# Sums over d as two row tiles of 64 partitions in three blocks of four, rows of x0 by transposes, and the fold of a block's partial sums split between GpSimd and VectorE

## The chip, the cores and the metric

The kernel runs on one core of a Trainium2 chip. The metric is the device time of one execution in microseconds (us). TensorE (PE in the rows, its weight loads PEld), VectorE (DVE), ScalarE (ACT), GpSimd (POOL) and the DMA queues each run their own program and meet through semaphores.

## The reference

A recommendation model: 39 embedding rows of 16 numbers for each of 512 samples go through a three-layer cross network, and then through a small perceptron.

```python
e = jnp.stack([tbl_0[ids[:, 0]], ..., tbl_38[ids[:, 38]]], axis=1)   # (512, 39, 16)
x0 = xk = e
for W in (f0, f1, f2):             # (39*39, 128), (128*39, 128), (128*39, 128)
    z = jnp.einsum('bfd,bgd->bfgd', x0, xk).reshape(b, f * g, d)
    cur = jnp.einsum('bpd,pm->bmd', z, W)
    outs.append(cur); xk = cur
z = jnp.sum(jnp.concatenate(outs, axis=1), axis=-1)                  # (512, 384)
h = jnp.concatenate([z, dense_ctx], axis=1)
h = jnp.maximum(h @ W_top1 + b_top1, 0.0)
h = jnp.maximum(h @ W_top2 + b_top2, 0.0)
y = h @ W_top3
```

## The kernel before

A **tile** is 32 samples times 16 values of d, 512 columns; there are 16 tiles. A tile has four **blocks** of 128 columns (8 samples times 16 d), 64 blocks in all. A block's second layer is ten **banks** (a bank is a PSUM buffer y2 of four fields, 512 columns; the tenth has three fields). Each bank is one **slot**, so a tile has 40 slots, numbered 0 to 39 here; slots 40, 41, ... are slots 0, 1, ... of the next tile. Every engine's program is written out along the same slots by hand: an operation's slot is its place in its engine's order, not a time.

In a slot TensorE runs the bank's three matmuls (lines 779 to 781). VectorE multiplies each field of the bank with the field's x0 and adds it to a running sum (line 682, four operations a bank), except for banks 0, 3 and 6 of a block, which ScalarE scales (line 526). There are four y2 buffers, so bank n waits until bank n - 4 has been read. Between the banks lie:

- the next tile's first layer: VectorE's products z = z * three_ps (line 652, at slots 0, 4, ..., 24), their low halves by GpSimd (line 426), TensorE's contraction into acc0 (lines 753, 754 and 759, at slots 8, 12, ..., 32), then x1_low (line 658) and sum_x1 (line 665) by VectorE at slots 35 and 36;
- the rows of x0: four matmuls against the identity a tile (line 743, slot 33), copied by ScalarE;
- the second layer's result of a block: GpSimd adds the three partial sums, fold_two at slot 8 of the block (line 434) and fold_three at slot 2 of the next block (line 441); VectorE adds the four fields of the sum, 128x512 to 128x128, by a reduction, x2_of (line 690) at slot 4 of the next block; TensorE then sums over d with s_block (line 786): the stationary operand is x2 (8 samples x 16 d on the partitions, 128 channels), the moving one is diag, 8 x 40 columns, in which the columns of sample b are nonzero only in b's 16 partitions. It writes 320 columns of the PSUM buffer side, which ScalarE copies to s_sb. s_block stands S_LAG = 18 slots behind its block's first bank, so at slots 8, 18, 28 and 38 of a tile;
- the third layer (line 797) and the perceptron (lines 808, 809, 818 and 825) of the group of four tiles before, from the fifth tile on; the perceptron falls into tiles 7, 11 and 15, counted from 0.

After the last bank the last block's fold, s_block, third layer and perceptron run one after the other.

Of the kernel before, what the change touches and what calls it, by code (L numbers as in the profile page):

```python
# [15 lines left out]
F = 39  # L16
# [5 lines left out]

COLS = 512
BLK = 8
GROUPS = B // P
TPG = 4
TILES = GROUPS * TPG
# [40 lines left out]
BY_ACT = (0, 3, 6)  # L68
FOLD_AT = 8
THIRD_AT = 2  # L70
X2_AT = 4


B_STEP = 4
FIRST_B_AT = 4
HIGH_LAG = 2
LOW_LAG = 3
CONTRACT_LAG = 8
X1_AT = 34
FIRST_X1_AT = 37  # L80
S_LAG = 18

LAST_BLOCKS = (TILES * SLOTS - 2 - S_LAG) // BANKS + 1
ROWS_AT = 33
# [82 lines left out]
    return k // BANKS if k >= 0 and k % BANKS == 0 else None  # L167


def small_fields(tables):  # L170
    return [f for f in range(F) if tables[f].shape[0] <= CHUNKS * ROWS]

# [22 lines left out]
def cross_network(nc, ids, ids_small, row_numbers, small_tables, tables, w0a, w0b, w1, w1_w, w2, wt1, bt1, wt2, bt2, wt3, dense_t, selectors, identity, mask8, out):  # L195
    with ExitStack() as ctx:
# [35 lines left out]

        scaled = sb("scaled", [P, 2, len(BY_ACT), FPB * M])
        sum4 = sb("sum4", [P, FPB * M])
        x2_sb = sb("x2_sb", [P, 2, M])
        diag = sb("diag", [P, 2, NBLK, BLK, FS])
        s_sb = sb("s_sb", [P, 2, FS, P])
# [58 lines left out]
        terms_in = sem("terms_in")  # L296
        y_act = sem("y_act")
        four_in = sem("four_in")
        x2_in = sem("x2_in")
        diag_in = sem("diag_in")  # L300
        s_ready = sem("s_ready")
# [97 lines left out]
        @block.gpsimd  # L399
        def _(pool):  # L400
            def single(g, i):
                f = SINGLES[i]
                if g >= 2 and i == 0:
                    pool.wait_ge(stored[0], 16 * STORES * (2 * (g - 1)))
                    pool.wait_ge(stored[1], 16 * STORES * (2 * (g - 1)))
                pool.indirect_dma_start(
                    out=emb_singles[:, g % 2, i, :], out_offset=None, in_=tables[f][:, :],
                    in_offset=bass.IndirectOffsetOnAxis(ap=ids_sb[:, g, f:f + 1], axis=0),
                ).then_inc(singles_in[g], 16)

            def quad(u, i):
                n = len(QUADS[i])
                if u >= 2 and i == 0:
                    pool.wait_ge(stored[u % 2], 16 * STORES * (u // 2))
                pool.indirect_dma_start(  # L415
                    out=emb_quads[0:SPT * n, u % 2, i, :], out_offset=None, in_=packed,
                    in_offset=bass.IndirectOffsetOnAxis(ap=quad_rows[0:SPT * n, u, i:i + 1], axis=0),
                ).then_inc(quad_in[i][u % 2], 16)

            def low_part(u, c):  # L420
                n = C0 * u + c
                pool.wait_ge(z_hi_in, n + 1)
                if n >= Z_RING:
                    pool.wait_ge(z_done, n - Z_RING + 1)
                k = depth(c)
                pool.tensor_tensor(z_lo[0:k, n % Z_RING, :], z[0:k, c, :], z_hi[0:k, n % Z_RING, :].bitcast(F32),  # L426
                                   ALU.subtract).then_inc(z_lo_in, 1)

            def fold_two(k):

                pool.wait_ge(terms_in, dve_terms(BANKS * k + BY_ACT[2] - 1))
                if k > 0:
                    pool.wait_ge(x2_in, k)
                pool.tensor_tensor(sum4[:, :], scaled[:, k % 2, 0, :], scaled[:, k % 2, 1, :],  # L434
                                   ALU.add).then_inc(four_in, 1)

            def fold_three(k):

                pool.wait_ge(terms_in, dve_terms(BANKS * k + BANKS - 1))
                pool.wait_ge(four_in, 2 * k + 1)  # L440
                pool.tensor_tensor(sum4[:, :], sum4[:, :], scaled[:, k % 2, 2, :], ALU.add).then_inc(four_in, 1)  # L441

            pool.wait_ge(ids_in, 16)
            for i in range(len(SINGLES)):
                single(0, i)
            pool.wait_ge(quads_first, 1)
            for i in range(len(QUADS)):
                quad(0, i)
            pool.wait_ge(rest_ids_in, 80)
            pool.wait_ge(quads_rest, 1)  # L450
            for i in range(4):
                quad(1, i)
            low_part(0, 2)
            quad(1, 4)
            low_part(0, 4)
            quad(1, 5)
            low_part(0, 6)
            for i in range(6, len(QUADS)):
                quad(1, i)
            for t in range(TILES):  # L460
                for s in range(SLOTS):
                    k, j = NBLK * t + s // BANKS, s % BANKS
                    c = chunk_at(t + 1, s, LOW_LAG)
                    if c is not None:
                        low_part(t + 1, c)
                    if j == FOLD_AT:
                        fold_two(k)
                    if j == THIRD_AT and k > 0:
                        fold_three(k - 1)
                    for alone, a, i in gathers_at(t, s):  # L470
                        if alone:
                            single(a, i)
                        else:
                            quad(a, i)
            fold_three(BLOCKS - 1)

        @block.scalar
        def _(act):
# [20 lines left out]
            def three(u):  # L499
                act.wait_ge(three_in[u % 2], 48 * (u // 2 + 1))  # L500
                if u > 0:
                    act.wait_ge(prod, C0 * u)
                copy(three_ps[0:3 * F, :], x0_three[0:3 * F, u % 2, :]).then_inc(three_up, 1)

            def high_part(u, c):
# [25 lines left out]
            def s_out(k):  # L531
                act.wait_ge(s_ready, k + 1)
                g, at = k // (TPG * NBLK), BLK * (k % (TPG * NBLK))
                if at == 0 and g >= 2:
                    act.wait_ge(r3_ready, g - 1)
                copy(s_sb[:, g % 2, :, at:at + BLK],
                     side[:, 0:BLK * FS].rearrange("p (b f) -> p f b", f=FS)).then_inc(s_in, 1)

            def r2_out(g):
                act.wait_ge(s_in, (g + 1) * TPG * NBLK)  # L540
# [88 lines left out]
        def _(dve):  # L629
# [54 lines left out]

            def x2_of(k):

                dve.wait_ge(four_in, 2 * k + 2)
                if k >= 2:
                    dve.wait_ge(s_ready, k - 1)
                dve.tensor_reduce(x2_sb[:, k % 2, :], sum4[:, :].rearrange("p (f m) -> p m f", f=FPB),  # L690
                                  AX_X, ALU.add).then_inc(x2_in, 1)

            def second_filter_low(i):
                cut = slice(W1_CUTS[i], W1_CUTS[i + 1])
# [27 lines left out]
            for t in range(TILES):  # L722
                for s in range(SLOTS):
# [9 lines left out]
                        sum_x1(t + 1)  # L733
                    if s % BANKS == X2_AT and n > BANKS:
                        x2_of(n // BANKS - 1)
            x2_of(BLOCKS - 1)

        @block.tensor
        def _(pe):
            def rows_of(u):  # L740
                pe.wait_ge(three_in[u % 2], 48 * (u // 2 + 1))
                for k in range(NBLK):
                    mm = pe.matmul(side[:, k * F:(k + 1) * F], x0_three[0:F, u % 2, k * P:(k + 1) * P],  # L743
                                   ident[0:F, 0:F], start=True, stop=True)
                mm.then_inc(rows_t, 1)

            def contract(u, c):
                n = C0 * u + c
                s, k = n % Z_RING, depth(c)
                if c == 0 and u > 0:  # L750
                    pe.wait_ge(r1_in, u)
                pe.wait_ge(z_hi_in, n + 1)
                pe.matmul(acc0[:, :], w0_hi[0:k, c, :], z_hi[0:k, s, :], start=c == 0, stop=False)  # L753
                pe.matmul(acc0[:, :], w0_lo[0:k, c, :], z_hi[0:k, s, :], start=False, stop=False)  # L754
# [28 lines left out]
            def s_block(k):  # L783
                pe.wait_ge(x2_in, k + 1)
                pe.wait_ge(diag_in, BLK * (k // NBLK + 1))
                pe.matmul(side[:, 0:BLK * FS], x2_sb[:, k % 2, :],  # L786
                          diag[:, k // NBLK % 2, k % NBLK, :, :].rearrange("p b f -> p (b f)"),
                          start=True, stop=True).then_inc(s_ready, 1)

            def layer3(g, fields):  # L790
                if 0 in fields:
# [188 lines left out]
```

## Time and profile before

| | |
|---|---|
| median of three runs | 735.24 us (734.88 to 735.31) |
| the profiled execution's own time | 735.52 us |
| its span, first to last instruction | 733.7 us |
| mean granted clock of TensorE | 0.991 of full speed |
| TensorE matmuls busy | 671.3 us (91%) |
| VectorE busy | 626.0 us (85%) |
| ScalarE busy | 390.5 us (53%) |
| GpSimd busy | 459.2 us (63%) |

The profile is of one execution, whose time is 1.8 us more than its span. Matmul durations overlap, since a matmul is recorded from its start to the end of its modelled pipeline: what one costs is read from the start of the next.

### The profile page before, as it was taken

Reading aid. Unit: us, or ns where it says so; the run is one execution under the profiler, and the core shown is the slowest. Engines: PE = TensorE matmul, PEld = TensorE weight load, DVE = VectorE, ACT = ScalarE, POOL = GpSimd, SP = SyncE. Lnnn points to the kernel's source line nnn. Section 1 sums busy time; section 2 is a strip of 40 time slices with the busy share of each in tenths; the row PEclk is TensorE's granted clock in tenths of the full one; section 3 lists DMA queues with packets and bytes.
Section 4 is the critical chain, followed back from the end, with each engine's and each line's share of the span. In section 5 each row is a group of like instructions: output and inputs, shape, how many; then the busy total and the mean of one; then the engine's idle time right before and its main releaser. Section 6 shows DMA issues by size and latency. Waiting matters only on the chain.

```text
span 733.7 us, 11667 instructions
## 1 busy us (share of the span) xinstructions
PE 671.3 (91%) x3072; PEld 523.1 (71%) x3072; DVE 626.0 (85%) x2018; ACT 390.5 (53%) x1163; POOL 459.2 (63%) x404
## 2 busy tenths in 40 slices
PE   0187989999999999999999999999999999999977
PEld 0165767676767778787867778787867778787856
DVE  3646999999999898999789898999789898999750
ACT  0325565665656565656456565656456565655321
POOL 6345979586868776775658776775658675552220
PEclk9998999999999999999999999999999999999989
DMA  9814640404040313112030312112040303000000
GB/s 145 155 37 123 208 107 8 106 6 105 7 106 7 97 17 78 34 47 66 5 105 7 99 14 77 35 42 70 5 106 5 104 10 88 16 1 0 1 1 0
DMA packets 70261, 41.27 MB, mean 56 GB/s; under 512 B 47298, under 2 KB 55042, under 8 KB 70067
## 3 DMA queue, kind: packets, MB, share of 16 engines
q1 hardware_dynamic: 60438, 36.45, 19.7%
q0 software_dynamic: 5248, 1.29, 2.1%
q10 hardware_dynamic: 4508, 2.80, 2.0%
q8 instruction: 24, 0.39, 0.2%
q14 instruction: 43, 0.34, 0.2%
HBM read 38.55 MB, written 1.94 MB: 55 GB/s over the span
## 4 chain that ended last, share of the span: by engine, by line
PE 67%; DVE 19%; issue 5%; DMA 3%; POOL 2%; ACT 2%; ACTq 1%; SPq 0%; DVEq 0%; POOLq 0%
PE y L779 17%; PE y L781 14%; PE y L780 14%; DVE scaled L682 14%; PE late L797 4%; PE side L786 3%; PE acc L754 3%; PE acc L753 3%; PE acc L759 3%; PE side L743 2%; DMA s_sb<-in_w_dram 2%; PE late L808 2%; DVE z L652 1%; PE late L830 1%; DVE x_parts L658 1%
## 5 line engine op out<-in xcount | busy, mean ns | idle before, releaser
L682 DVE SCALAR_TENSOR_TENSOR scaled<-y,x_rows,scaled 128x128 f32<-128x128 f32 x1728 | 465.4, 342 | 53.5 <-PE y L781 35.6
L526 ACT ACTIVATE scaled<-y,x_rows 128x128 f32<-128x128 f32 x768 | 218.8, 367 | 165.0 <-PE y L781 150.3
L779 PE MATMUL y<-w_hi,x_parts 128*128 128x512 f32 (+1 forms) x640 | 277.7, 434 | 18.2 <-DVE scaled L682 8.8
L781 PE MATMUL y<-w_hi,x_parts 128*128 128x512 f32 (+1 forms) x640 | 249.0, 389 | 0.0
L780 PE MATMUL y<-w_lo,x_parts 128*128 128x512 f32 (+1 forms) x640 | 248.6, 389 | 0.0
L426 POOL TENSOR_TENSOR z_parts<-z,z_parts 117x512 fp32r<-117x512 f32 (+1 forms) x108 | 139.5, 1291 | 88.8 <-ACT z_parts L480 67.1
L779 PEld LDWEIGHTS y<-w_hi,x_parts 128*128 128x128 f32 x640 | 120.8, 189 | 80.8 <-DVE scaled L682 50.6
L415 POOL DMA_INDIRECT emb_quads<-in_small_tables_dram,quad_rows x144 | 138.0, 959 | 32.7 <-issue 15.5
L781 PEld LDWEIGHTS y<-w_hi,x_parts 128*128 128x128 f32 x640 | 120.7, 189 | 24.9
L434 POOL TENSOR_TENSOR sum<-scaled 128x512 f32<-128x512 f32 x64 | 82.8, 1293 | 84.0 <-DVE scaled L682 83.6
L780 PEld LDWEIGHTS y<-w_lo,x_parts 128*128 128x128 f32 x640 | 121.5, 190 | 14.2
L480 ACT ACTIVATE z_parts<-z 117x512 fp32r<-117x512 f32 (+1 forms) x112 | 71.0, 635 | 74.5 <-DVE z L652 72.0
L441 POOL TENSOR_TENSOR sum<-sum,scaled 128x512 f32<-128x512 f32 x64 | 83.1, 1299 | 36.8 <-DVE scaled L682 36.3
L652 DVE TENSOR_TENSOR z<-z,three_ps 117x512 f32<-117x512 f32 (+1 forms) x112 | 75.6, 677 | 0.0
L690 DVE TENSOR_REDUCE x_sb<-sum 128x128 f32<-128x512 f32 x64 | 68.7, 1073 | 2.3 <-POOL sum L441 2.1
L797 PEld LDWEIGHTS late<-s_sb,w_sb 128*128 128x128 f32 x312 | 53.9, 195 | 11.7 <-ACT s_sb L480 1.5
L797 PE MATMUL late<-s_sb,w_sb 128*128 128x128 f32 x312 | 55.5, 281 | 0.5 <-ACT s_sb L480 0.5
L786 PE MATMUL side<-diag,x_sb 128*128 128x320 f32 x128 | 45.6, 437 | 4.5 <-issue 4.5
L496 ACT ACTIVATE diag<-x_rows,mask_sb 32x160 f32<-32x160 f32 x128 | 48.6, 416 | 1.2
L480 ACT ACTIVATE s_sb<-side 128x320 f32<-128x320 f32 x64 | 27.8, 435 | 36.0 <-PE side L786 35.6
L753 PE MATMUL acc<-z_parts,w_hi 117*128 117x512 f32 (+1 forms) x112 | 44.4, 396 | 0.9 <-ACT z_parts L480 0.9
L759 PE MATMUL acc<-z_parts,w_hi 117*128 117x512 f32 (+1 forms) x112 | 44.2, 395 | 0.7 <-POOL z_parts L426 0.7
(42 smaller groups left out, 352.0 us busy)
## 6 DMA issues: line engine op xcount, KB each, us to landing
z<-x_turned SPq DMA_DIRECT2D x309, 78.0 KB
x_three<-x_turned SPq DMA_DIRECT2D x48, 78.0 KB
x_turned<-emb_quads SPq DMA_DIRECT2D x160, 8.0 KB
w_sb<-in_w_dram SPq DMA_DIRECT2D x1, 2496.0 KB, 9.6
emb_quads<-in_small_tables_dram,quad_rows POOLq DMA_INDIRECT x144, 2.4
x_turned<-emb_singles SPq DMA_DIRECT2D x96, 2.0 KB
s_sb<-in_w_dram ACTq DMA_DIRECT2D x9, 160.0 KB, 8.4
z<-x_turned ACTq DMA_DIRECT2D x11, 78.0 KB
```

Of the source, the lines that this page charges most:

```text
L415: pool.indirect_dma_start(out=emb_quads[0:SPT * n, u % 2, i, :], out_offset=None, in_=packed, in_offset=bass.IndirectOffsetOnAxis(ap=quad_ ...
L426: pool.tensor_tensor(z_lo[0:k, n % Z_RING, :], z[0:k, c, :], z_hi[0:k, n % Z_RING, :].bitcast(F32), ALU.subtract).then_inc(z_lo_in, 1)
L434: pool.tensor_tensor(sum4[:, :], scaled[:, k % 2, 0, :], scaled[:, k % 2, 1, :], ALU.add).then_inc(four_in, 1)
L441: pool.tensor_tensor(sum4[:, :], sum4[:, :], scaled[:, k % 2, 2, :], ALU.add).then_inc(four_in, 1)
L480: return act.activation(dst, src, ACT.Copy)
L526: done = act.activation(scaled[:, k % 2, BY_ACT.index(j), i * M:(i + 1) * M], y2[n % RING][:, i * M:(i + 1) * M], ACT.Copy, scale=x0_rows[ ...
L652: dve.tensor_tensor(z[0:k, c, :], z[0:k, c, :], three_ps[0:k, :], ALU.mult).then_inc(prod, 1)
L682: dve.scalar_tensor_tensor(part, y2[n % RING][:, i * M:(i + 1) * M], x0_f, part, ALU.mult, ALU.add).then_inc(terms_in, 1)
L779: pe.matmul(dst, x1_hi[:, t % 2, cols], hi, start=True, stop=False)
L780: pe.matmul(dst, x1_hi[:, t % 2, cols], lo, start=False, stop=False)
L781: pe.matmul(dst, x1_lo[:, t % 2, cols], hi, start=False, stop=True).then_inc(y_ready, 1)
L797: mm = pe.matmul(late[:, 0:P], w2_sb[:, f, :], s_sb[:, g % 2, f, :], start=f == 0, stop=f == F - 1)
```

## The change

The fold: GpSimd adds the two halves of the 128x512 sum after fold_three (a new 128x256 addition into sum2), and x2_of becomes one 128x128 addition of sum2's halves on VectorE; it moves from slot 4 of a block to slot 5. For the last block VectorE does all three additions (last_x2). The sum over d: in three blocks of four (those whose s_block stands at slot 27, 37 or 7 of a tile, in tiles 1 to 15) samples 0 to 3 are summed by a matmul over partitions 0 to 63 with 160 columns into side, and samples 4 to 7 by one over partitions 64 to 127 with 160 columns into another bank (three_ps or acc0, which are free then); ScalarE copies the two parts one after the other. S_LAG goes from 18 to 17, so s_block stands at slots 7, 17, 27 and 37. The rows of x0 are made by four transposes in place of four matmuls with the identity. The contraction, x1_high, x1_low and sum_x1 move back by one slot.

```diff
@@ -68,17 +69,17 @@
 BY_ACT = (0, 3, 6)
 FOLD_AT = 8
 THIRD_AT = 2
-X2_AT = 4
+X2_AT = 5
...
 HIGH_LAG = 2
 LOW_LAG = 3
-CONTRACT_LAG = 8
-X1_AT = 34
+CONTRACT_LAG = 9
+X1_AT = 35
 FIRST_X1_AT = 37
-S_LAG = 18
+S_LAG = 17
...
+
+
+def second_half(k):
+
+
+    t, s = divmod(k * BANKS + S_LAG, SLOTS)
+    if t == 0 or t == TILES:
+        return None
+    return "acc0" if s < BANKS else "three_ps" if s > 2 * BANKS else None
...
@@ -439,6 +451,8 @@
                 pool.wait_ge(terms_in, dve_terms(BANKS * k + BANKS - 1))
                 pool.wait_ge(four_in, 2 * k + 1)
                 pool.tensor_tensor(sum4[:, :], sum4[:, :], scaled[:, k % 2, 2, :], ALU.add).then_inc(four_in, 1)
+                pool.wait_ge(four_in, 2 * k + 2)
+                pool.tensor_tensor(sum2[:, :], sum4[:, 0:2 * M], sum4[:, 2 * M:4 * M], ALU.add).then_inc(two_in, 1)
...
                 act.wait_ge(three_in[u % 2], 48 * (u // 2 + 1))
                 if u > 0:
                     act.wait_ge(prod, C0 * u)
+                if u > 2:
+                    act.wait_ge(s_in, NBLK * (u - 2) + 3)
                 copy(three_ps[0:3 * F, :], x0_three[0:3 * F, u % 2, :]).then_inc(three_up, 1)
...
-                     side[:, 0:BLK * FS].rearrange("p (b f) -> p f b", f=FS)).then_inc(s_in, 1)
+                if second_half(k) is None:
+                    copy(s_sb[:, g % 2, :, at:at + BLK],
+                         side[:, 0:BLK * FS].rearrange("p (b f) -> p f b", f=FS)).then_inc(s_in, 1)
+                else:
+                    copy(s_sb[:, g % 2, :, at:at + HALF],
+                         side[:, 0:HALF * FS].rearrange("p (b f) -> p f b", f=FS))
+                    src = {"acc0": acc0, "three_ps": three_ps}[second_half(k)]
+                    copy(s_sb[:, g % 2, :, at + HALF:at + BLK],
+                         src[:, 0:HALF * FS].rearrange("p (b f) -> p f b", f=FS)).then_inc(s_in, 1)
...
             def x2_of(k):
 
-                dve.wait_ge(four_in, 2 * k + 2)
+                dve.wait_ge(two_in, k + 1)
                 if k >= 2:
                     dve.wait_ge(s_ready, k - 1)
-                dve.tensor_reduce(x2_sb[:, k % 2, :], sum4[:, :].rearrange("p (f m) -> p m f", f=FPB),
-                                  AX_X, ALU.add).then_inc(x2_in, 1)
+                dve.tensor_tensor(x2_sb[:, k % 2, :], sum2[:, 0:M], sum2[:, M:2 * M], ALU.add).then_inc(x2_in, 1)
...
+            def last_x2(k):
+
+                dve.wait_ge(terms_in, dve_terms(BANKS * k + BANKS - 1))
+                dve.wait_ge(four_in, 2 * k + 1)
+                dve.tensor_tensor(sum4[:, :], sum4[:, :], scaled[:, k % 2, 2, :], ALU.add).then_inc(four_in, 1)
+                dve.wait_ge(four_in, 2 * k + 2)
+                dve.tensor_tensor(sum2[:, :], sum4[:, 0:2 * M], sum4[:, 2 * M:4 * M], ALU.add).then_inc(two_in, 1)
+                x2_of(k)
...
                 for k in range(NBLK):
-                    mm = pe.matmul(side[:, k * F:(k + 1) * F], x0_three[0:F, u % 2, k * P:(k + 1) * P],
-                                   ident[0:F, 0:F], start=True, stop=True)
+                    mm = pe.transpose(side[:, k * F:(k + 1) * F], x0_three[0:F, u % 2, k * P:(k + 1) * P], ident[0:F, 0:F])
...
                     pe.wait_ge(r1_in, u)
+                if c == 0 and u > 1:
+                    pe.wait_ge(s_in, NBLK * (u - 1))
...
-                pe.matmul(side[:, 0:BLK * FS], x2_sb[:, k % 2, :],
-                          diag[:, k // NBLK % 2, k % NBLK, :, :].rearrange("p b f -> p (b f)"),
-                          start=True, stop=True).then_inc(s_ready, 1)
+                spread = diag[:, k // NBLK % 2, k % NBLK, :, :].rearrange("p b f -> p (b f)")
+                half = HALF * FS
+                if second_half(k) is None:
+                    pe.matmul(side[:, 0:BLK * FS], x2_sb[:, k % 2, :], spread, start=True, stop=True).then_inc(s_ready, 1)
+                else:
+                    if second_half(k) == "three_ps":
+                        pe.wait_ge(prod, C0 * min((k * BANKS + S_LAG) // SLOTS + 2, TILES))
+                    else:
+                        pe.wait_ge(r1_in, (k * BANKS + S_LAG) // SLOTS + 1)
+                    to = {"acc0": acc0, "three_ps": three_ps}[second_half(k)]
+                    pe.matmul(side[:, 0:half], x2_sb[0:P // 2, k % 2, :], spread[0:P // 2, 0:half], start=True, stop=True)
+                    pe.matmul(to[:, 0:half], x2_sb[P // 2:P, k % 2, :], spread[P // 2:P, half:2 * half],
+                              start=True, stop=True).then_inc(s_ready, 1)
```

How the change moves instructions, where the prediction speaks of it. The names are the tensors' without their suffixes: x_sb is x2_sb, sum is sum4 or sum2, x_parts is x1_parts, y_0 to y_3 are the four y2 buffers.

TensorE in tile 1, slots 37 and 38, before: s_block stands behind slot 38's bank.

```order
L781 MATMUL y_1<-w_hi,x_parts 128x512
L779 MATMUL y_2<-w_hi,x_parts 128x512 [waits terms_in]
L780 MATMUL y_2<-w_lo,x_parts 128x512
L781 MATMUL y_2<-w_hi,x_parts 128x512
L786 MATMUL side<-diag,x_sb 128x320 [waits diag_in,x2_in,rows_in]
L779 MATMUL y_3<-w_hi,x_parts 128x384 [waits terms_in]
```

The same place in the changed kernel.

```order
L812 MATMUL y_1<-w_hi,x_parts 128x512
L827 MATMUL side<-diag,x_sb 128x160 [waits diag_in,prod,x2_in,rows_in]
L828 MATMUL three_ps<-diag,x_sb 128x160
L810 MATMUL y_2<-w_hi,x_parts 128x512 [waits terms_in]
L811 MATMUL y_2<-w_lo,x_parts 128x512
L812 MATMUL y_2<-w_hi,x_parts 128x512
L810 MATMUL y_3<-w_hi,x_parts 128x384 [waits terms_in]
```

Slot 38's bank, which stood in front of s_block, now stands behind it, and the block's one matmul is two.

VectorE in tile 0, the last contraction products and a block's reduction, before (slots 24 and 25 of the tile).

```order
L682 SCALAR_TENSOR_TENSOR scaled<-y_0,x_rows,scaled 128x128 x3
L652 TENSOR_TENSOR z<-z,three_ps 117x512 [waits a_in_5]
L690 TENSOR_REDUCE x_sb<-sum 128x128 [waits four_in]
L682 SCALAR_TENSOR_TENSOR scaled<-y_1,x_rows,scaled 128x128 [waits terms_in,y_ready]
L682 SCALAR_TENSOR_TENSOR scaled<-y_1,x_rows,scaled 128x128 [waits terms_in] x3
L682 SCALAR_TENSOR_TENSOR scaled<-y_3,x_rows,scaled 128x128 [waits y_act,y_ready]
```

The same place in the changed kernel.

```order
L704 SCALAR_TENSOR_TENSOR scaled<-y_0,x_rows,scaled 128x128 x3
L674 TENSOR_TENSOR z<-z,three_ps 117x512 [waits a_in_5]
L704 SCALAR_TENSOR_TENSOR scaled<-y_1,x_rows,scaled 128x128 [waits terms_in,y_ready]
L704 SCALAR_TENSOR_TENSOR scaled<-y_1,x_rows,scaled 128x128 [waits terms_in] x3
L712 TENSOR_TENSOR x_sb<-sum 128x128 [waits two_in]
L704 SCALAR_TENSOR_TENSOR scaled<-y_3,x_rows,scaled 128x128 [waits y_act,y_ready]
```

One more bank of four operations stands in front of the x2 of a block.

## Rows read from the trace of the kernel before

**Rows 1.** The page's first lines: busy time, share, instructions.
```profile
PE 671.3 (91%) x3072; PEld 523.1 (71%) x3072; DVE 626.0 (85%) x2018; ACT 390.5 (53%) x1163; POOL 459.2 (63%) x404
```

**Rows 2.** Busy us by stretch: length; PE, PEld, DVE, ACT, POOL; clock; DMA share; GB/s.
```profile
170.40:209.40 39.00, 37.91 (x158) 27.52 (x158) 37.55 (x122) 23.15 (x70) 27.74 (x25) 1.00 0.22 51
...
288.90:328.40 39.50, 39.02 (x182) 31.32 (x182) 37.49 (x122) 23.39 (x70) 27.40 (x25) 1.00 0.23 56
...
328.40:374.50 46.10, 45.53 (x225) 36.33 (x225) 37.69 (x121) 25.43 (x79) 27.96 (x25) 1.00 0.23 55
```

**Rows 3.** Groups by shape: busy us, mean ns, idle before, releasers.
```profile
L441 POOL TENSOR_TENSOR sum<-sum,scaled 128x512 f32<-128x512 f32 x64 | 83.1, 1299 | 36.8 <-DVE scaled L682 36.3
L690 DVE TENSOR_REDUCE x_sb<-sum 128x128 f32<-128x512 f32 x64 | 68.7, 1073 | 2.3 <-POOL sum L441 2.1
...
L644 DVE TENSOR_TENSOR z_parts<-z,z_parts 117x512 fp32r<-117x512 f32 x4 | 2.8, 690 | 7.1 <-ACT z_parts L480 6.9
...
L706 DVE TENSOR_REDUCE mask_sb<-ident 128x8 f32<-128x128 f32 x1 | 0.3, 286 | 0.0
```

**Rows 4.** Chain of waits in 209.4:249.1 us: start, length, what.
```profile
232.40 0.22 PE late L797 x2
...
234.01 0.54 PE side L786 x2
```

**Rows 5.** Chain of waits in 345:374.5 us.
```profile
352.22 0.67 PE late L808 x6
352.89 0.41 PE late L809 x2
353.30 0.43 PE y L779
353.73 0.23 PE y L780
```

**Rows 6.** Timeline, TensorE around the rows of x0, tile 5's slot 33.
```profile
288.49 0.40 PE L781 MATMUL y<-w_hi,x_parts 128*128 128x512 f32 x1
...
288.81 0.96 PEld L743 LDWEIGHTS side<-ident,x_three 39*128 39x128 f32 x8 [0.36 <-issue]
...
289.82 0.19 PEld L779 LDWEIGHTS y<-w_hi,x_parts 128*128 128x128 f32 x1
```

**Rows 7.** Timeline, VectorE, tile 5's slot 34 to tile 6's slot 5.
```profile
290.82 1.12 DVE L682 SCALAR_TENSOR_TENSOR scaled<-y,x_rows,scaled 128x128 f32<-128x128 f32 x4 [1.49 <-PE y L781]
291.87 1.06 DVE L690 TENSOR_REDUCE x_sb<-sum 128x128 f32<-128x512 f32 x1
...
302.31 1.08 DVE L690 TENSOR_REDUCE x_sb<-sum 128x128 f32<-128x512 f32 x1
```

**Rows 8.** Timeline, TensorE: third matmuls of slots 37, 47 and 49.
```profile
292.70 0.40 PE L781 MATMUL y<-w_hi,x_parts 128*128 128x512 f32 x1
...
302.00 0.39 PE L781 MATMUL y<-w_hi,x_parts 128*128 128x512 f32 x1
...
304.94 0.34 PE L781 MATMUL y<-w_hi,x_parts 128*128 128x384 f32 x1
```

**Rows 9.** Timeline, slots 24 and 27 of tile 5: VectorE, TensorE.
```profile
280.96 0.68 DVE L652 TENSOR_TENSOR z<-z,three_ps 78x512 f32<-78x512 f32 x1
281.55 1.08 DVE L690 TENSOR_REDUCE x_sb<-sum 128x128 f32<-128x512 f32 x1
...
282.11 0.40 PE L781 MATMUL y<-w_hi,x_parts 128*128 128x512 f32 x1
```

**Rows 10.** Timeline behind the last bank.
```profile
707.02 1.26 POOL L441 TENSOR_TENSOR sum<-sum,scaled 128x512 f32<-128x512 f32 x1 [1.56 <-DVE scaled L682]
708.31 1.02 DVE L690 TENSOR_REDUCE x_sb<-sum 128x128 f32<-128x512 f32 x1 [1.37 <-POOL sum L441]
...
709.43 1.40 PE L786 MATMUL side<-diag,x_sb 128*128 128x320 f32 x2 [4.48 <-issue]
```

**Rows 11.** Timeline, GpSimd's low part at slot 47.
```profile
303.48 1.27 POOL L426 TENSOR_TENSOR z_parts<-z,z_parts 117x512 fp32r<-117x512 f32 x1 [1.75 <-DVE x_sb L690]
```

More of the change, by code:

```diff
@@ L24 @@
 BLK = 8
+HALF = BLK // 2
 GROUPS = B // P
@@ L234, in cross_network @@
         sum4 = sb("sum4", [P, FPB * M])
+        sum2 = sb("sum2", [P, 2 * M])
         x2_sb = sb("x2_sb", [P, 2, M])
@@ L298, in cross_network @@
         four_in = sem("four_in")
+        two_in = sem("two_in")
         x2_in = sem("x2_in")
@@ L474, in _ @@
                             quad(a, i)
-            fold_three(BLOCKS - 1)
         @block.scalar
@@ L535, in s_out @@
                     act.wait_ge(r3_ready, g - 1)
-                copy(s_sb[:, g % 2, :, at:at + BLK],
-                     side[:, 0:BLK * FS].rearrange("p (b f) -> p f b", f=FS)).then_inc(s_in, 1)
+                if second_half(k) is None:
[7 more added lines that the diff above has]
+                         src[:, 0:HALF * FS].rearrange("p (b f) -> p f b", f=FS)).then_inc(s_in, 1)
             def r2_out(g):
@@ L735, in _ @@
                         x2_of(n // BANKS - 1)
-            x2_of(BLOCKS - 1)
+            last_x2(BLOCKS - 1)
         @block.tensor
```

## Prediction

> **What bounds the kernel now.** I read the page's first line, then each engine's busy time tile by tile, then the chain of waits of single tiles, then the timeline at the places the change touches. TensorE is busy 91% and VectorE 85% of the span [rows 1]; neither share says which one bounds. By stretch the reader sees more: from slot 33 of one tile to slot 33 of the next it takes 39.0 us in the first four tiles, 39.5 us with the third layer beside it, and 46.1 us in the three tiles that also hold the perceptron, while VectorE is busy 37.5 to 37.7 us in all of them [rows 2]. So VectorE nearly sets the pace in tiles 0 to 3, both are close in nine tiles, and TensorE sets it in three. GpSimd has 27.4 to 28.0 us of work a tile, and is not near the bound. The timeline shows where the two trade places: VectorE runs without a gap from slot 34 to slot 44 (its reduction starts at 291.87 us and the next at 302.31 us [rows 7]), since the x1 work and two products fall there while TensorE has no contraction; behind that TensorE is the one that never waits.
>
> **What the change costs and gives, part by part.**
>
> *The reduction.* VectorE's 128x512 reduction takes 1073 ns, of which about 1.0 us is on its path. The new 128x128 addition is not in the trace. Below, a quarter of the 690 ns of a 512-column addition gives 0.17 us; above, the 128-column reduction took 286 ns [rows 3]. I take 0.3 us, the form with the same 128 columns. VectorE thus has 0.7 to 0.8 us less in each block, 3 us a tile. GpSimd's extra 256-column addition costs half to all of its 1.30 us for 512 columns [rows 3]; I take 0.65 us, 2.6 us a tile. It lies in GpSimd's idle time (27.4 to 28 of 39.5 us [rows 2]), and x2_of stands a bank later, which is about 1.1 us [rows 7] of new room. Without that cover x2_of would come 0.65 us later.
>
> *The two row tiles.* A full block's s_block takes 0.54 us, two passes of 320 columns, 0.27 us each [rows 4]. Passes of 160 columns are then 0.135 us, and there are four: 0.54 us one behind the other, 0.27 us if the halves run side by side. But a matmul with few rows also costs at both its ends. Two passes with 16 rows took 0.41 us and the matmul after them 0.43 us, where two passes with 128 rows take 0.22 us and a usual bank matmul 0.23 us [rows 4, 5]: 0.39 us for going in and out. The rows of x0, 39 partitions deep, show why: the bank's third matmul starts at 288.49 us and streams for 0.23 us, and the first load of the rows starts only at 288.81 us; at the end the bank's next load starts at 289.82 us, behind the eight pairs, while elsewhere a load is pulled ahead under the running matmul [rows 6]. So 0.2 us in and 0.2 us out.
> The Trainium skill, page TensorEngine Tiling (Array Packing), section Key Properties, says that changing the tiling mode, not just the tile, drains TensorE; these rows agree, and it speaks against putting one pair of row tiles among full matmuls.
> With the ends, a half-and-half block costs 0.54 + 0.4 = 0.94 us if the passes are serial and 0.67 us if they are fully side by side. I take 0.89 us: the second half's first pass can't start before its weights, which come one load (0.11 us: eight in 0.96 us, the last one 0.19 us long [rows 6]) behind each of the two before it. That is 0.35 us more than now; bounds +0.13 and +0.40. Where TensorE waits for x2 anyway, 0.1 us of going in is hidden.
>
> *The transposes.* Rows of x0 are eight load-and-matmul pairs in 0.96 us [rows 6], 0.11 us each. If a transpose goes in one pass there are four: 0.45 us less in 15 tiles, -6.75 us. If it needs two passes it saves nothing. I take one; the ends cost as before.
>
> *The distance between x2 and s_block.* Before, VectorE made x2 at slot 4 and TensorE used it at slot 8, four slots on, as far as the four y2 buffers let it run ahead. Now it is slot 5 and slot 7. Behind the waiting s_block stand all of TensorE's banks, and behind them VectorE and ScalarE. I put the new order on the old times:
> - Slot 37. VectorE begins bank 35 at 291.87 us instead of the reduction, ends it 1.0 us later and x2 0.3 us later: about 293.2 us. TensorE has streamed slot 37 at 292.70 + 0.23 = 292.93 us [rows 7, 8]. It waits 0.3 us, which VectorE's lead then uses up anyway.
> - Slot 47. From one x2 start to the next VectorE has 10.44 us now [rows 7]; with 0.3 for 1.0 us it is 9.7 us, so x2 is ready at 292.9 + 9.7 + 0.3 = 302.9 us, and TensorE, which would be done with slot 47 before 302.3 us [rows 8], waits. s_block ends 0.8 us later, slots 48 and 49 (0.7 + 0.5 us) and a third-layer pair (0.2 us) bring it to 305.2 us, where it is done with slot 49 at 305.1 us now (304.94 us plus 0.17 us [rows 8]), but with the contraction of slot 49, 0.7 us, still to do, which now is already done at slot 48. So each of the 15 turns from one tile to the next loses 0.7 us: VectorE's relief in this stretch is given back, since TensorE's lead was cut by two slots, +10.5 us.
> - Slot 27. The product ends 0.6 us behind 280.96 us, then come bank 25 (1.0 us) and x2: 282.6 to 282.9 us with the relief upstream. TensorE has slot 27 at 282.34 us [rows 9]: 0.3 us of wait, and 0.35 - 0.1 us of s_block, 0.55 us in the nine tiles with a third layer and no perceptron, +4.95 us. In the three perceptron tiles TensorE comes late and pays only 0.35 us, +1.05 us. In tiles 1 to 3 what VectorE gains in the middle of the tile pays for it, all but 0.05 us, +0.15 us.
> - Slot 17 has a full block and a contraction before it: nothing. Tile 15 has one more half-and-half block in a stretch that TensorE bounds, +0.35 us.
>
> *The end.* GpSimd's addition (from 707.02 us) and the reduction are followed by s_block at 709.43 us [rows 10]. Three additions on VectorE of 0.69, 0.4 and 0.3 us with small steps between take 1.65 us: -0.75 us. The copies of s_sb in two pieces and the contraction's slot lie under ScalarE's idle time (23 of 39 us busy [rows 2]); uncovered, they would delay the contraction of slot 9 by 0.2 us.
>
> *Sum.* -6.75 + 10.5 + 4.95 + 1.05 + 0.15 + 0.35 - 0.75 = +9.5 us. On the profiled execution's 735.5 us this is 745.0 us; the median of the runs is 0.3 us below that execution: 744.7 us, said as 744.5.
>
> **The rivals.**
> - *VectorE's relief wins.* Its 3 us a tile reach the end, if TensorE's lead at slots 27 to 47 is enough after all and the halves run side by side. For it: VectorE is busy 37.6 of 39.0 us in tiles 0 to 3 [rows 2]. Against it: the gapless stretch of rows 7. It gives -6.75 (transposes) + 45 x 0.13 (row tiles) - 4 x 1.5 (first tiles) - 12 x 0.6 (the others) - 0.75 = -15 us, 720.5 us. It decides if x2 of slot 45 is ready before TensorE has done slot 47. Chance 0.30.
> - *The parts cancel.* Side-by-side halves at +0.13 us and a turn that loses 0.3 us: -6.75 + 5.9 + 4.5 - 0.75 - 2 = +1 us, 736 us. Chance 0.12.
> - *VectorE and GpSimd get in each other's way.* The reduction reads one SBUF operand, the new addition two. At slot 47 GpSimd's low part starts at 303.48 us [rows 11], half a microsecond behind my time for x2 of slot 45, and takes 1.27 us; if the addition had to wait for such an operation, up to 1.27 us would lie right on the path of 15 turns: at half of that, +9.5 us more, 754 us. No row shows a two-operand addition of VectorE held up so (the four of line 644 took their 690 ns [rows 3]), and the order of the two is close. Chance 0.18.
> The Trainium skill, page SBUF — State Buffer, section Who interferes with whom, says that a VectorE instruction with two SBUF inputs contends with a GpSimd instruction that reads SBUF, and that tensor_reduce never does; no run here shows it yet.
>
> **How the numbers follow.** The forecast has 0.40. About 0.2% (1.5 us) is what a measurement of this kernel tells from no change. Faster: the first rival and a little of the second, 0.32; within 0.2%: 0.08; slower: the forecast, the third rival and part of the second, 0.60. The forecast's own range is 735 (halves side by side, -9.9 us) to 752 us (two-pass transposes, +6.75). Both signs hold much, so the range of all cases is 721 to 757 us: it leaves out half of the first rival and the worst of the third.
>
> **What the profile after would show.** Right: TensorE waits for x2 at slots 7, 27 and 37 in the waits, the bank matmul behind a half-and-half block 0.2 us longer, s_block about 0.9 us in the chain, four transposes in 0.5 us, x2_of near 0.3 us, tiles 4 to 6 at 40 us or more. Wrong: tiles of 38.5 us and less; no wait in front of s_block; the second half's passes starting with the first's; a transposed row that costs as much as before; x2_of at 1 us or more (then the third rival). What would upset the forecast most is VectorE's stretch between slots 35 and 45 being shorter than the 9.7 us I carried over.

## The result and the profile after

The changed kernel takes 760.39 us (median of four runs, 758.88 to 761.82) against 735.06 us for the kernel before in the same session: a ratio of 1.035, 95% interval 1.032 to 1.038, so 25 us slower. The forecast had the sign, but its 744.5 us was 16 us short and its range ended at 757 us.

The page's first lines, and the rows of who waited for whom for s_block's loads and for the load of a bank's first matmul (engine, line, releaser: us in total, times, longest):

```profile
span 757.0 us, 11873 instructions
...
PE 656.1 (87%) x3098; PEld 512.1 (68%) x3098; DVE 605.2 (80%) x2020; ACT 395.3 (52%) x1208; POOL 504.5 (67%) x466
...
PEld side L827 <- issue: 49.5, 45, 1.8
...
PEld side L820 <- issue: 28.5, 18, 3.3
...
PEld y L810 <- DVE scaled L704: 16.6, 62, 0.7
```

TensorE lost 15 us of work and VectorE 21 us against [rows 1], and the span is 23 us longer: nothing has become the bound by its own load, the two engines wait for each other. TensorE's loads wait 78 us in front of s_block. In the kernel before such waits were 5.3 us in four places of a load, and one of 4.5 us of a matmul. The kernel is not 78 us longer, because other waits shrank: the load of a bank's first matmul waited 50.6 us for VectorE before and 16.6 us now. The row from the kernel before:

```profile
PEld y L779 <- DVE scaled L682: 50.6, 109, 1.0
```

By stretch, from slot 33 of tiles 2, 5 and 6, to be put beside [rows 2] (length; PE, PEld, DVE, ACT, POOL):

```profile
174.50:215.00 40.50, 36.09 (x161) 27.36 (x160) 36.23 (x122) 23.68 (x73) 30.62 (x29) 1.00 0.20 51
297.50:339.00 41.50, 38.41 (x185) 30.41 (x184) 36.47 (x122) 23.70 (x73) 30.57 (x28) 1.00 0.22 55
339.00:386.60 47.60, 44.70 (x226) 35.27 (x225) 36.23 (x121) 25.57 (x81) 30.36 (x29) 1.00 0.21 56
```

Every kind of tile is 1.5 to 2.0 us longer by these rows, though VectorE has 1.0 to 1.5 us less to do in each. The groups by shape that answer to [rows 3]:

```profile
L455 POOL TENSOR_TENSOR sum<-sum 128x256 f32<-128x256 f32 x63 | 46.4, 736 | 4.9
L712 DVE TENSOR_TENSOR x_sb<-sum 128x128 f32<-128x128 f32 x64 | 37.5, 586 | 0.8 <-POOL sum L455 0.7
L827 PE MATMUL side<-diag,x_sb 64*128 64x160 f32 x90 | 22.9, 334 | 31.5 <-issue 31.4
L773 PE MATMUL side<-ident,x_three 39*128 39x39 f32 x64 | 7.0, 234 | 0.0
```

The 128x128 addition has a mean of 586 ns, and a mean of two kinds: the view of its line alone says minimum, median and maximum.

```profile
L712 DVE TENSOR_TENSOR x_sb<-sum x64: 272/281/1815, 74.4 to 733.0; 128x128 f32<-128x128 f32 x64
```

The typical one takes the 0.28 us that was assumed; 16 of the 64 took 0.5 to 1.8 us, 15 of them at slot 15, one in each tile but the last. The timeline of slots 15 to 17 of tile 5 (start, length, engine) shows what holds it:

```profile
279.79 0.74 POOL L455 TENSOR_TENSOR sum<-sum 128x256 f32<-128x256 f32 x1
280.02 0.40 PE L812 MATMUL y<-w_hi,x_parts 128*128 128x512 f32 x1
...
280.49 1.27 POOL L438 TENSOR_TENSOR z_parts<-z,z_parts 117x512 fp32r<-117x512 f32 x1
...
280.56 1.34 DVE L712 TENSOR_TENSOR x_sb<-sum 128x128 f32<-128x128 f32 x1 [0.24 <-POOL sum L455]
...
281.83 0.67 DVE L674 TENSOR_TENSOR z<-z,three_ps 117x512 f32<-117x512 f32 x1
...
281.98 0.30 PEld L820 LDWEIGHTS side<-diag,x_sb 128*128 128x128 f32 x2 [1.29 <-issue]
```

GpSimd ends the sum of halves and starts its low part at 280.49 us; VectorE's addition starts at 280.56 us and ends 0.15 us behind GpSimd's, at 281.90 us. TensorE's s_block of slot 17 starts at 281.98 us, where it could have started behind the contraction at 280.95 us: 1.03 us lost. Read the same way, the loss at slot 17 is 1.0 to 1.8 us in each of the tiles 1 to 13.

At slot 27 the s_block is a pair of row tiles (timeline of tile 5 again, TensorE's matmuls, then its loads):

```profile
291.23 0.40 PE L812 MATMUL y<-w_hi,x_parts 128*128 128x512 f32 x1
292.03 0.37 PE L827 MATMUL side<-diag,x_sb 64*128 64x160 f32 x1 [0.40 <-issue]
292.04 0.40 PE L828 MATMUL three_ps<-diag,x_sb 64*128 64x160 f32 x1
292.24 0.30 PE L827 MATMUL side<-diag,x_sb 64*128 64x160 f32 x1
292.28 0.30 PE L828 MATMUL three_ps<-diag,x_sb 64*128 64x160 f32 x1
...
292.00 0.18 PEld L827 LDWEIGHTS side<-diag,x_sb 64*128 64x128 f32 x1 [0.81 <-issue]
...
292.50 0.19 PEld L810 LDWEIGHTS y<-w_hi,x_parts 128*128 128x128 f32 x1 [0.17 <-DVE scaled L704]
292.61 0.19 PEld L811 LDWEIGHTS y<-w_lo,x_parts 128*128 128x128 f32 x1
```

The halves do run side by side, 0.01 to 0.04 us apart. From the end of the wait at 292.00 us to the load of L811, which is pulled ahead when the bank's first matmul starts streaming, are 0.61 us; with a full block the same stretch is 0.64 us (281.98 to 282.62 us). Slot 27 is done at 291.23 + 0.23 = 291.46 us, so the wait is 0.54 us; at slot 37 it is 0.33 us and at slot 7 of that tile 1.49 us, read the same way. The transposes are four, and the next bank's load comes 0.37 us behind the first (298.54 and 298.91 us) where it came 1.01 us behind [rows 6].

### The profile page after: what moved, and what is told of

Its sections match the earlier page's. It is cut to its first block, busy times and chain, and to the rows that moved or that the text cites. A ratio compares the mean times of both kernels' runs of the same rounds, so it can differ in the third digit from the quotient of the medians.

```text
span 757.0 us, 11873 instructions
## 1 busy us (share of the span) xinstructions
PE 656.1 (87%) x3098; PEld 512.1 (68%) x3098; DVE 605.2 (80%) x2020; ACT 395.3 (52%) x1208; POOL 504.5 (67%) x466
## 4 chain that ended last, share of the span: by engine, by line
PE 77%; issue 9%; DVE 7%; DMA 3%; ACT 2%; ACTq 1%; POOL 1%; SPq 0%; DVEq 0%; POOLq 0%
PE y L810 19%; PE y L812 17%; PE y L811 17%; DVE scaled L704 6%; PE late L838 5%; PE acc L784 3%; PE acc L785 3%; PE acc L790 3%; PE side L827 2%; PE side L820 2%; DMA s_sb<-in_w_dram 2%; PE late L849 2%; PE late L871 1%; ACTq L342 1%; PE late L859 1%
## 5 line engine op out<-in xcount | busy, mean ns | idle before, releaser
L704 DVE SCALAR_TENSOR_TENSOR scaled<-y,x_rows,scaled 128x128 f32<-128x128 f32 x1728 | 473.5, 343 | 100.9 <-ACT scaled L541 53.6
L810 PE MATMUL y<-w_hi,x_parts 128*128 128x512 f32 (+1 forms) x640 | 272.8, 426 | 7.9 <-ACT scaled L541 4.4
L811 PE MATMUL y<-w_lo,x_parts 128*128 128x512 f32 (+1 forms) x640 | 249.0, 389 | 0.0
L810 PEld LDWEIGHTS y<-w_hi,x_parts 128*128 128x128 f32 x640 | 121.0, 189 | 48.4 <-DVE scaled L704 16.6
L811 PEld LDWEIGHTS y<-w_lo,x_parts 128*128 128x128 f32 x640 | 121.7, 190 | 17.1
L674 DVE TENSOR_TENSOR z<-z,three_ps 117x512 f32<-117x512 f32 (+1 forms) x112 | 75.6, 677 | 0.0
L509 ACT ACTIVATE diag<-x_rows,mask_sb 32x160 f32<-32x160 f32 x128 | 50.2, 418 | 1.5
L827 PE MATMUL side<-diag,x_sb 64*128 64x160 f32 x90 | 22.9, 334 | 31.5 <-issue 31.4
L455 POOL TENSOR_TENSOR sum<-sum 128x256 f32<-128x256 f32 x63 | 46.4, 736 | 4.9
L827 PEld LDWEIGHTS side<-diag,x_sb 64*128 64x128 f32 x90 | 13.3, 185 | 49.5 <-issue 49.5
L784 PE MATMUL acc<-z_parts,w_hi 117*128 117x512 f32 (+1 forms) x112 | 44.4, 397 | 0.9 <-ACT z_parts L493 0.9
L785 PE MATMUL acc<-z_parts,w_lo 117*128 117x512 f32 (+1 forms) x112 | 44.3, 396 | 0.0
```

The costliest lines, as they stand in the source:

```text
L674: dve.tensor_tensor(z[0:k, c, :], z[0:k, c, :], three_ps[0:k, :], ALU.mult).then_inc(prod, 1)
L704: dve.scalar_tensor_tensor(part, y2[n % RING][:, i * M:(i + 1) * M], x0_f, part, ALU.mult, ALU.add).then_inc(terms_in, 1)
L810: pe.matmul(dst, x1_hi[:, t % 2, cols], hi, start=True, stop=False)
L811: pe.matmul(dst, x1_hi[:, t % 2, cols], lo, start=False, stop=False)
```

## The experiments

Two theories. Theory 1: VectorE's new addition reads two SBUF operands and is held up by a GpSimd operation. Theory 2: the distance between x2 and its s_block, cut from four slots to two, turns TensorE's lead into waits. The rivals stand in the expectations. Medians are of four or five runs; the ratio is to the kernel before in the same session (735.5 to 736.3 us). Unless a line says otherwise, a kernel is the changed one with the edit shown.

**One operand.**

```diff
-                dve.tensor_tensor(x2_sb[:, k % 2, :], sum2[:, 0:M], sum2[:, M:2 * M], ALU.add).then_inc(x2_in, 1)
+                dve.tensor_reduce(x2_sb[:, k % 2, :], sum2[:, :].rearrange("p (f m) -> p m f", f=2),
+                                  AX_X, ALU.add).then_inc(x2_in, 1)
```

> The changed kernel, with VectorE's 128x128 addition of sum2's two halves made by a reduction over one operand (128x256 to 128x128) in place of an addition of two. Theory 1 (the new addition, with two SBUF operands, is held up by a GpSimd operation that reads SBUF, once a tile, at slot 15: 16 of its 64 took 1.1 to 1.8 us, the others 0.28 us): all 64 reductions take 0.5 to 0.6 us, none over 0.7 us; the 15 long ones go, 1.05 us each on TensorE's path, and about 0.27 us is added at slots 5, 25 and 35, of which two thirds lie on the path: 760 - 16 + 8 = 752 us. Theory 2 (all of the loss is the shorter distance from x2 to s_block, the long additions only fill time in which VectorE would wait anyway): 760 + 8 = 768 us.

Measured: 751.87 us, ratio 1.022 (1.020 to 1.024), 8.5 us less, as Theory 1 expected; a reduction takes 0.41 to 0.43 us, where 0.5 to 0.6 was expected. The line's view:

```profile
L712 DVE TENSOR_REDUCE x_sb<-sum x64: 407/415/431, 74.8 to 723.3; 128x128 f32<-128x256 f32 x64
```

No long one is left, at the same place in the same order, although each is 0.14 us longer than a free addition; the tiles with the third layer go from 41.4 to between 40.6 and 40.9 us. Theory 1 holds for its share. That share is larger than 8.5 us: from slot 9 to slot 19, where slot 15's addition stood, tiles 1 to 15 take 15.0 us less than in the changed kernel, and the 0.14 us more in each reduction lengthens the other stretches (table in the next section).

**x2_of one slot earlier.**

```diff
-X2_AT = 5
+X2_AT = 4
```

> The changed kernel with x2_of back at slot 4 of a block (X2_AT 5 to 4), all else as it is, so three slots lie between x2 and its s_block in place of two. Theory 2 (the distance): the waits before s_block shrink by one bank's time of VectorE, 1.04 us at slot 7, 0.5 us at slot 27 and 0.3 us at slot 37, 15 times: 760 - 28 = 732 to 740 us. Theory 1 (only the held-up addition): the long addition comes one slot earlier, as long as before, TensorE has a slot more for it: -0.7 us a tile and no more, 750 us.

Measured: 728.12 us, ratio 0.989 (0.987 to 0.991). This one slot is worth 32 us, more than expected, and turns the loss into a gain. Loads wait 24.4 + 12.7 us in front of s_block, for 78 before. But the edit also moves the additions against GpSimd's operations: seven of 64 take 1.33 to 1.36 us and nine 0.44 to 0.78 us, where 15 took over 1 us before, so the 32 us are not all distance; the next run separates the two. One of the seven is tile 5's:

```profile
273.67 1.27 POOL L438 TENSOR_TENSOR z_parts<-z,z_parts 117x512 fp32r<-117x512 f32 x1
273.74 1.34 DVE L712 TENSOR_TENSOR x_sb<-sum 128x128 f32<-128x128 f32 x1 [1.28 <-POOL sum L455]
```

At slot 27 nothing waits here, so it shows what row tiles cost by themselves:

```profile
284.42 0.40 PE L812 MATMUL y<-w_hi,x_parts 128*128 128x512 f32 x1
284.74 0.40 PE L827 MATMUL side<-diag,x_sb 64*128 64x160 f32 x1
284.75 0.40 PE L828 MATMUL three_ps<-diag,x_sb 64*128 64x160 f32 x1
...
285.22 0.50 PE L810 MATMUL y<-w_hi,x_parts 128*128 128x512 f32 x1
285.55 0.40 PE L811 MATMUL y<-w_lo,x_parts 128*128 128x512 f32 x1
```

L811 follows L810's stream by 0.23 us, so that stream starts at 285.32 us, 0.67 us behind the end of slot 27's (284.65 us), where a full block takes 0.54 us [rows 4].

**Both.** The two edits together.

> The changed kernel with x2_of at slot 4 and as a reduction over one operand (the two edits before together). Theory 1 (the two-operand addition is held up by GpSimd; in the kernel with x2_of at slot 4 ten of the 64 took 1.3 us and eight 0.6 to 0.8 us): the long ones go, about 0.9 us in seven or more tiles, against 0.14 us more in each of the others, half of it on the path: 728 - 7 + 3 = 724 us. If the long additions there lie beside other waits, the result is 728 to 731 us.

Measured: 722.83 us, ratio 0.982 (0.981 to 0.984): 5 us less than with x2_of a slot earlier alone. (The expectation counted ten and eight long additions; the trace has seven and nine.) With the reduction no addition is held up at either distance, so 751.87 to 722.83 us is the distance alone: 29 us.

**Full blocks, at two and at three slots.** The second kernel has X2_AT = 4 as well.

```diff
-    if t == 0 or t == TILES:
-        return None
-    return "acc0" if s < BANKS else "three_ps" if s > 2 * BANKS else None
+    return None
```

> The changed kernel with all 64 blocks summed over d by one full matmul of 320 columns, as in the kernel before; lags, transposes and fold as in the changed kernel. The forecast's step (a block in two row tiles costs 0.35 us more than a full one): 45 x 0.35 = 16 us less, 745 us. The trace after (0.61 us from the end of the wait to the next bank's stream with row tiles, 0.64 us with a full block): within 2 us of the changed kernel, 760 to 763 us.

> The changed kernel with x2_of at slot 4 and all blocks summed by one full matmul, S_LAG 17. Against the run with x2_of at slot 4 it is the row tiles alone, in a kernel in which TensorE hardly waits in front of them. The forecast's step (0.35 us a block): 728 - 15 = 713 us. The forecast's lower bound, and what slot 27 shows in that run (1.37 us to the next bank against 0.70, so 0.67 us against 0.54): 45 x 0.13 = 6 us less, 722 us. If row tiles are worth what they were made for: over 729 us.

Measured: 762.23 us, ratio 1.036 (1.033 to 1.039), against 1.035 with row tiles; and 724.82 us, ratio 0.986 (0.984 to 0.988), against 0.989 (0.987 to 0.991). In a kernel that waits in front of s_block the row tiles are worth nothing either way. With x2 earlier the full block's median is 3.3 us lower, where 6 us were expected, but the intervals overlap, so no gain is shown. Both runs refute the forecast's 0.35 us a block (745 and 713 us were expected by it).

**Four slots, full blocks.** X2_AT = 4, S_LAG = 18, full blocks as above, and without the two waits that guard acc0 and three_ps.

> The changed kernel with x2_of at slot 4, S_LAG back at 18 and all blocks summed by one full matmul (so the waits that guard acc0 and three_ps are not needed and are left out); transposes, GpSimd's addition and VectorE's 128x128 addition as in the changed kernel. Four slots from x2 to s_block as in the kernel before. Theory 2 (distance): the waits before s_block that are left at three slots (PEld 24 + 13 us in the run with x2_of at slot 4, of which some 0.3 us a tile beyond what a full ring costs) go, and the full blocks save 0.13 us each where nothing waits: 728 - 4 - 6 = 718 us. If three slots are as good as four: 722 us. If the half-and-half blocks were a gain after all: over 730 us.

Measured: 718.82 us, ratio 0.978 (0.976 to 0.980). With full blocks and the two-operand addition the kernel takes 762.2 us at two slots, 724.8 us at three and 718.8 us at four. The step from two to three, 37 us, holds both causes: 15 additions took over 1 us at two slots (maximum 1.92 us), seven at three. The 29 us with the reduction are the distance alone. The step from three to four, 6 us, has seven such additions on either side.

**The same with the reduction.**

> As the run with four slots and full blocks, and x2_of as a reduction over one operand. Both theories together: no long x2_of is left (in the run before it six of 64 took 1.33 to 1.37 us and seven 0.5 to 0.8 us in tiles with the third layer), against 0.14 us more in the others: 719 - 6 + 2 = 715 us. If TensorE now has enough lead to cover a held-up addition: 719 to 721 us.

Measured: 715.89 us, ratio 0.973 (0.971 to 0.975), 3 us less, as both theories together expected. Against the reduction at two slots (751.87 us) four slots are worth 36 us, row tiles or full blocks counted as equal.

**The contraction back as well.** CONTRACT_LAG = 8 and X1_AT = 34 in the kernel above.

> As the run with four slots, full blocks and the reduction, with the contraction, x1_high, x1_low and sum_x1 back at the slots of the kernel before (CONTRACT_LAG 8, X1_AT 34). Neither theory gives the shift of these a weight: within 1.5 us of the run beside it. If GpSimd's low parts, which now have GpSimd's additional 0.74 us a block before them, come too late for a contraction a slot earlier, 1 to 2 us more in every tile, 730 us or more.

Measured: 712.34 us, ratio 0.968 (0.966 to 0.970), which is 3.5 us below the kernel above and outside the expected 1.5 us. It is the fastest kernel of the study, 3.2% faster than the one before. What it keeps of the change is the transposes, GpSimd's addition of halves and a short operation for x2.

**The old fold at three slots.** x2_of at slot 4 as the reduction of all of sum4, without sum2 on either engine.

> The changed kernel with x2_of at slot 4, but with the old fold: VectorE's 128x512 reduction of sum4 and no addition of halves on GpSimd; row tiles, transposes and S_LAG 17 stay. It shows what VectorE's relief is worth and what three slots cost without it. The relief is 0.75 us a block: if VectorE's stretch behind slot 34 sets the pace, 15 tiles x about 1.5 us more than with the new fold: 750 us. If only the slots matter and the relief is lost in TensorE's pace: 730 us.

Measured: 745.79 us, ratio 1.015 (1.013 to 1.017): the new fold is worth 18 us in this order, and 23 us against the one with the reduction (722.83 us), in which nothing is held up either. That agrees with VectorE setting the pace behind slot 34.

**The distance alone.** The kernel before with two lines changed.

```diff
-X2_AT = 4
+X2_AT = 5
-S_LAG = 18
+S_LAG = 17
```

> The kernel before with x2_of at slot 5 and s_block at slots 7, 17, 27 and 37 (X2_AT 5, S_LAG 17), and nothing else: the distance alone. Theory 2: each x2 is ready 0.75 us later than with the new fold, which comes on top of waits of 1.5, 0.5 and 0.3 us at slots 7, 27 and 37: 3 us a tile and more, 770 to 785 us. Rival: four y2 buffers cover it, since each of them bounds TensorE's lead at the same places anyway: under 740 us.

Measured: 817.8 us, ratio 1.111 (1.108 to 1.114), 82 us slower, well beyond what was expected. No two-operand addition makes x2 here, so the distance is enough for a loss. Loads wait in front of s_block, in us, times and longest; the other row is the page's busy time:

```profile
PE 677.8 (83%) x3072; PEld 535.4 (66%) x3072; DVE 635.3 (78%) x2018; ACT 390.2 (48%) x1163; POOL 459.2 (56%) x404
...
PEld side L786 <- issue: 116.8, 63, 4.2
```

TensorE's same 3072 matmuls are busy for 677.8 us, 6.5 us more than before [rows 1], and its mean granted clock is 0.975, for 0.991 before. So some of the 82 us is clock, in a kernel in which TensorE waits more, and not the wait itself; how much of it lies on the path is not shown.

**The transposes alone**, in the kernel before.

> The kernel before with the rows of x0 made by four transposes a tile, and nothing else. The forecast's step: 15 x 0.45 = 6.75 us less, 728.3 us. By the trace after (0.37 us from the first to the next bank's load, in place of 1.01 us): 15 x 0.64 = 9.6 us less, 725.5 us. Rival: VectorE's gapless stretch behind slot 34 sets the pace, and TensorE only waits there for longer: less than 3 us gained.

Measured: 729.23 us, ratio 0.991 (0.990 to 0.993), 7.1 us less than the 736.33 us beside it. The saving by rows is 9.6 us; 7.1 us came through.

## Why the prediction was right or wrong

*The distance: right in mechanism and in the times of x2.* On the old times, with slot 33's third matmul (288.49 us before, 297.51 us after) laid upon each other, x2 of slot 35 was forecast for 293.2 us and came at 302.27 - 9.02 = 293.25 us; x2 of slot 45 was forecast for 302.9 us and came at 311.95 - 9.02 = 302.93 us. TensorE's waits were 1.49 us at slot 7, 0.54 us at slot 27 (0.3 us forecast) and 0.33 us at slot 37 (0.3 us). The two times of x2:

```profile
301.99 0.28 DVE L712 TENSOR_TENSOR x_sb<-sum 128x128 f32<-128x128 f32 x1
...
311.67 0.28 DVE L712 TENSOR_TENSOR x_sb<-sum 128x128 f32<-128x128 f32 x1
```

The runs at two, three and four slots show the cause. What the turn costs was forecast too high, though: see the table.

*The step that failed: "Slot 17 has a full block and a contraction before it: nothing."* It cost 1.03 us in tile 5. The addition that makes x2, costed at 0.3 us, took 1.34 us there. The table has the change's cost by stretch, read between the starts of the third matmuls of the slots named, changed kernel less kernel before, in us over all tiles; 0.69 us is taken out for a contraction (three matmuls, 0.23 us each) that stands in one of the two only.

| stretch | forecast | measured | with the reduction |
|---|---|---|---|
| slots 9 to 19, tiles 1 to 15 | 0 | +17.3 | +2.3 |
| slots 19 to 29, tiles 1 to 15 | +6.5 | +9.6 | +11.4 |
| slots 29 to 33, tiles 1 to 15 | 0 | -0.6 | -0.6 |
| the 15 turns, slots 33 to 49, with the transposes | +3.75 | -1.9 | +2.6 |

So the hold-up at slot 15 is the one step that carries the miss: with the reduction its stretch costs 15.0 us less. The prediction had the mechanism as its third rival with a chance of 0.18, and looked for it at slot 45, where GpSimd's low part stood close by; there VectorE's addition came first by 0.1 us and took 0.28 us. What decides is where GpSimd's operations stand at slot 15. In tiles 1, 5 and 9 its low part is queued behind the new sum of halves, and x2_of starts just behind that sum. In ten other tiles the sum had ended earlier; x2_of started while GpSimd ended an indirect DMA, its low part began 0.16 to 0.26 us later, and the addition was held all the same. The Trainium skill's page SBUF — State Buffer, section Who interferes with whom, says that a VectorE instruction with two SBUF inputs contends with a GpSimd instruction that reads SBUF. The trace agrees in all the additions that started behind a GpSimd addition or subtraction: each ended 0.15 to 0.16 us behind it. The same section of the Trainium skill says that issue order decides who blocks; that is not borne out by the recorded starts of these ten, see below. Adding only the hold-up to the forecast (744.5 + 15.0 = 759.5 us) comes within 1 us of the measured time, and that is luck: the turns came 5.7 us cheaper than forecast, slots 19 to 29 came 3.1 us dearer, 0.7 us were lost before the first turn, and 1.7 us gained behind slot 33 of the last tile.

*The row tiles: mis-sized.* Forecast +0.35 us a block (+0.25 us behind a wait), measured +0.13 us without a wait (0.67 against 0.54 us) and -0.03 us behind one (0.61 against 0.64 us). The total without a wait is what 0.27 us side by side and 0.2 us at either end give, but the rows have 0.24 us between the two passes of a half and 0.34 us from the second to the next stream, so this split isn't shown. The step "the second half's first pass can't start before its weights, which come one load ... behind each of the two before it" was wrong: the second half's load and matmul started 0.01 to 0.04 us behind the first's. The forecast's lower bound was the right value.

*The transposes: right, and larger.* 0.64 us a tile, for 0.45 us forecast: the pairs come 0.06 us apart, not 0.11 us. Alone they gave 7.1 us, for 6.75 us forecast.

*Slots 19 to 29, and the first tiles.* Slots 19 to 29 of tile 5 take 0.6 us more than before once the contraction's shift is taken out, for 0.55 us forecast, by two errors that nearly cancel: the wait was longer (0.54 for 0.3 us) and the pair cheaper. In tiles 1 to 3 nothing of VectorE's relief was kept: 40.5 us for 39.0 us, with 0.75 us more in slots 19 to 29, where 0.05 us was forecast.

*The end.* Three additions on VectorE take 731.78 to 733.26 us, 0.69, 0.43 and 0.29 us long, and s_block starts 1.55 us behind the first one's start; 1.65 us was forecast.

```profile
731.78 0.69 DVE L718 TENSOR_TENSOR sum<-sum,scaled 128x512 f32<-128x512 f32 x1
732.51 0.43 DVE L720 TENSOR_TENSOR sum<-sum 128x256 f32<-128x256 f32 x1
732.97 0.29 DVE L712 TENSOR_TENSOR x_sb<-sum 128x128 f32<-128x128 f32 x1
733.33 0.30 PEld L820 LDWEIGHTS side<-diag,x_sb 128*128 128x128 f32 x2 [3.32 <-issue]
```

*What stays open.* In the run with the distance alone, which keeps the old reduction and has two slots, the loss was 82 us, about twice what adding 0.75 us to each wait gives; its tile is 4.9 us longer. In tile 5 its loads of s_block start 2.2, 0.7, 1.3 and 1.6 us behind the end of the stream before them at slots 7, 17, 27 and 37 (1.5, 1.0, 0.5 and 0.3 us in the changed kernel), so each wait grows but slot 17's; why by so much is not shown. Why the contraction's slot is worth 3.5 us was not tried further. Whether the transposes' 0.64 us a tile reaches the end in the changed kernel, or goes into the wait at slot 7, no run separates; the forecast counted it in full beside a turn that VectorE sets.

## What to carry to other kernels

When two engines feed each other through a ring of buffers, the distance in the program between a producer's step and the in-order wait for it is a buffer too: cutting it from four slots to two cost 36 us with the reduction, more than everything else in this change gave, and it must be checked at each place where the producer is behind, not against its mean load. Make a short operation short in its operands too: an addition of two SBUF operands on VectorE that follows a GpSimd result can meet GpSimd's next addition, which held it for up to 1.5 us here; the same sum as a reduction of one operand took 0.41 to 0.43 us every time. Two row tiles in two banks do run side by side, but going in and out of them costs about as much as the second pass that they save, so one pair at a time doesn't pay here; whether a run of many would was not tried.

## What the runs showed of the hardware that was not expected

- VectorE's two-operand addition is held until 0.15 to 0.16 us behind the end of a GpSimd addition or subtraction that was running when it started: all 37 of this kind in three kernels (the changed one, x2_of at slot 4, and four slots with full blocks), 0.44 to 1.37 us long, their length set only by how much of GpSimd's operation was left. Beside an indirect DMA that GpSimd issues, additions took 0.28 us.
- Additions recorded 0.10 to 0.17 us ahead of GpSimd's start took 0.28 us, but ten in the changed kernel that started 0.16 to 0.26 us ahead of it, with a GpSimd indirect DMA just ending, took 1.59 to 1.69 us, to 0.16 us behind the end of GpSimd's operation; an eleventh, 0.38 us ahead, took 1.82 us. The indirect DMA alone is not the reason: in the kernel with four slots and full blocks two additions started 0.21 and 0.22 us ahead, also with an indirect DMA just ending, and took 0.28 us. What the eleven share, and none of the others that started ahead has, is the next instruction on VectorE, the product z = z * three_ps (L674); behind the others comes an operation on a bank or x1_low. No run tests this, and why the earlier one lost stays open. The pair below, from tile 2, is one of the ten.

```profile
157.52 1.69 DVE L712 TENSOR_TENSOR x_sb<-sum 128x128 f32<-128x128 f32 x1
...
157.78 1.27 POOL L438 TENSOR_TENSOR z_parts<-z,z_parts 117x512 fp32r<-117x512 f32 x1
```

- A transpose of 39x128 fp32 took one load and one matmul, 0.06 us apart from the next, where the same product as a matmul took two pairs of 0.11 us.
